# Channel-mix and convolution scan: group statistics over 64 rows at once, rows normalised four at a time

## The reference

```
x = x + mix(gn(x))          # gn: group norm, 32 groups of 2 channels, eps 1e-5
x = x + scan(gn(x))

mix:  posmap = softmax over n of pos_score[m, n, s]        # 4 heads s
      out[b,w,m,v,s] = sum_n posmap[m,n,s] * x[b,w,n,v,s]  + token_bias[m]
scan: out[0] = row[0]
      out[h] = row[h] + relu(conv1d(out[h-1], W))          # h = 1..63, 9 taps, 64 -> 64 channels
```

## Time and profile before

| | us |
|---|---|
| median of 3 runs (875.48 to 876.52) | 876.46 |
| the profiled execution | 875.68 |
| its span in the trace | 873.6 |
| PE / PEld busy | 799.9 / 732.1 |
| ACT busy | 642.9 |
| DVE busy | 618.7 |
| POOL busy | 435.7 |

### The profile page before, as it was taken

One profiled execution on the slowest core, in us unless ns is written; L12 is line 12 of the kernel. 1 busy time (PEld: TensorE's weight loads), 2 busy tenths in 40 slices (PEclk: granted clock), 3 DMA queues, 4 the chain that ended last, 5 costly groups with the idle time before them and its releaser, 6 DMA issues.

```text
span 873.6 us, 20141 instructions
## 1 busy us (share of the span) xinstructions
PE 799.9 (92%) x5734; PEld 732.1 (84%) x5734; DVE 618.7 (71%) x1536; ACT 642.9 (74%) x1462; POOL 435.7 (50%) x416
## 2 busy tenths in 40 slices
PE   1778887888799999999999999997999999999997
PEld 1555555555599999999899999997999999999997
DVE  7677778777578888989797978765555555555553
ACT  2477777777758887888788888887677677677664
POOL 1665655566265655566566665662333333333333
PEclk9999999999999999999999999999999999999999
DMA  9334343433134444444434343221222222223223
GB/s 186 68 74 96 74 96 72 90 78 83 38 74 93 90 97 98 98 90 94 90 84 91 87 96 74 49 50 37 62 62 67 66 60 67 65 60 68 64 60 72
DMA packets 203159, 68.18 MB, mean 78 GB/s; under 512 B 137556, under 2 KB 203092, under 8 KB 203092
## 3 DMA queue, kind: packets, MB, share of 16 engines
q1 hardware_dynamic: 203092, 67.43, 35.0%
HBM read 33.85 MB, written 33.55 MB: 77 GB/s over the span
## 4 chain that ended last, share of the span: by engine, by line
PE 71%; issue 9%; ACT 7%; DVE 7%; POOL 3%; ACTq 1%; DMA 1%; SPq 1%; DVEq 0%; POOLq 0%
PE ps_conv L898 30%; PE ps_conv L902 15%; PE ps_mix L812 8%; PE ps_mix L814 6%; PE ps_out L890 5%; ACT x_paired L424 5%; PE ps_in L827 5%; PE ps_small L801 2%; POOL xs L341 2%; POOL total L364 1%; DVE carry L732 1%; DVE x_sb L642 1%; DVE st L553 1%; DVE st L649 1%; DMA x_sb<-in_x_dram 1%
## 5 line engine op out<-in xcount | busy, mean ns | idle before, releaser
L364 POOL TENSOR_TENSOR total<-x_paired,carry 128x256 f32<-128x256 f32 x256 | 193.5, 757 | 299.6 <-DVE carry L732 293.5
L341 POOL TENSOR_TENSOR xs<-x_sb,rstd 128x512 f32<-128x512 f32 x128 | 232.9, 1846 | 93.6 <-DVE rstd L624 66.8
L424 ACT ACTIVATE x_paired<-ps_in,shift 64x256 f32 (+1 forms) x512 | 237.9, 465 | 7.8 <-POOL total L364 1.2
L740 DVE TENSOR_TENSOR carry_l<-carry,carry_h 128x256 fp32r<-128x256 f32 x252 | 177.0, 703 | 86.3 <-ACT carry_h L483 83.7
L898 PE MATMUL ps_conv<-carry_h,wh 128*128 128x256 f32 x1280 | 219.7, 303 | 4.7 <-ACT carry_h L483 4.7
L463 ACT ACTIVATE rows<-x_paired,shift,rstd 128x128 f32 (+1 forms) x512 | 221.3, 481 | 0.9 <-DVE shift L672 0.7
L483 ACT ACTIVATE carry_h<-carry 128x256 fp32r<-128x256 f32 x252 | 105.8, 420 | 140.9 <-DVE carry L732 139.0
L898 PE MATMUL ps_conv<-carry_h,wl 128*128 128x256 f32 x1280 | 197.7, 285 | 0.0
L902 PE MATMUL ps_conv<-carry_l,wh 128*128 128x256 f32 x1280 | 196.8, 284 | 0.0
L898 PEld LDWEIGHTS ps_conv<-carry_h,wh 128*128 128x128 f32 x1280 | 176.9, 192 | 7.2 <-ACT carry_h L483 5.6
L898 PEld LDWEIGHTS ps_conv<-carry_h,wl 128*128 128x128 f32 x1280 | 174.0, 190 | 0.0
(11 more groups left out here) (73 smaller groups left out, 354.9 us busy)
## 6 DMA issues: line engine op xcount, KB each, us to landing
x_sb<-in_x_dram SPq DMA_DIRECT2D x64, 512.0 KB, 4.0
out_dram<-staged SPq DMA_DIRECT2D x256, 128.0 KB, 2.4
x_paired<-in_L_conv_W_dram SPq DMA_DIRECT2D x2, 80.0 KB, 2.7
x_paired<-in_L_conv_W_dram SPq DMA_DIRECT2D x2, 64.0 KB, 2.4
x_paired<-v_attention_centers_dram SPq DMA_DIRECT2D x1, 0.0 KB
x_paired<-v_attention_spreads_dram SPq DMA_DIRECT2D x1, 0.0 KB
bias_col<-v_token_proj_n_bias_dram SPq DMA_DIRECT2D x1, 0.5 KB, 5.3
```

What stands on the lines that cost most here:

```text
L341: nc.gpsimd.tensor_tensor(xs[:, c % 2, heads, :, :], src, rstd1[:, m:G:2].unsqueeze(1).unsqueeze(1).to_broadcast([P, CG, CR, V]), ALU.mult ...
L364: nc.gpsimd.tensor_tensor(total[s][:, :].rearrange("p (w j) -> p w j", w=WS), x1_rows(wave, it, i, 1, s * WS, WS)[:, 0, :, :], carry[s][:, ...
L424: ins = nc.scalar.activation(dst[q * C:(q + 1) * C, r:HR:2, :], src[:, q, :, :], ACT.Identity, bias=shift1[r * C:(r + 1) * C, e:e + 1])
L740: nc.vector.tensor_tensor(carry_l[s][:, :, EDGE:EDGE + J], carry[s][:, :].rearrange("p (w j) -> p w j", w=WS), carry_h[s][:, :, EDGE:EDGE ...
```

## The change

Statistics of `x` are taken over all 64 rows in 16 operations of 256 elements; all stand in steps 4 and 5, two in each gap, and for image 0 behind the softmax. The tiles lose their dimension of halves, each average on PE has one source instead of two, and the matrix holds 1/128 instead of 1/256. Rows are normalised four at a time (`RG` = 4): one operation of 256 elements behind each `carry_h` instead of two of 128, and `rows` holds twice as much. The load of chunk 3 moves from step 2 to step 1.

```diff
-    RG = 2
+    RG = 4
-    HALF_COUNT = H // 2 * CG
+    COUNT = H * CG
...
-                    if i in (0, 2) and more >= 1:
-                        load_chunk(b + 1, 1 - e, 2 + i // 2)
+                    if i in (0, 1) and more >= 1:
+                        load_chunk(b + 1, 1 - e, 2 + i)
...
-                            for k in range(2):
-                                norm_rows(wave, it + g // GROUPS, g % GROUPS, (i % RG) * 2 * NS + 2 * s + k)
+                            norm_rows(wave, it + g // GROUPS, g % GROUPS, (i % RG) * NS + s)
...
-            def stats1(b, e, half, first, count):
-
-                for c in (2 * half, 2 * half + 1):
+            def stats1(b, e, first, count):
+
+                for c in range(CH):
                     dve.wait_ge(x_loaded[e][c], 8 * (b - e) + 16)
-                v = x_sb[:, e, 2 * half * CC:2 * (half + 1) * CC]
-                v = v.rearrange("p (h m g e) -> p m h e g", m=G // 2, g=2, e=CG)
+                v = x_sb[:, e, :].rearrange("p (h m g e) -> p m h e g", m=G // 2, g=2, e=CG)
                 for m in range(first, first + count):
-                    ins = nc.vector.bn_stats(st1[:, half, 2 * m:2 * m + 2, :].rearrange("p g k -> p (g k)"),
+                    ins = nc.vector.bn_stats(st1[:, 2 * m:2 * m + 2, :].rearrange("p g k -> p (g k)"),
                                              v[:, m, :, :, :])
-                if half == 1 and first + count == G // 2:
+                if first + count == G // 2:
                     ins.then_inc(stats1_done, 1)
...
-            stats1(0, 0, 0, 0, G // 2)
             dve.wait_ge(prob_ready, S)
...
-            stats1(0, 0, 1, 0, G // 2)
+            stats1(0, 0, 0, G // 2)
...
-                nc.vector.tensor_tensor(dev[:, :, :], st1[:, :, :, 1],
-                                        mean1.unsqueeze(1).to_broadcast([P, 2, G]),
-                                        ALU.subtract).then_inc(dev_ready, 1)
+                nc.vector.tensor_tensor(dev[:, :], st1[:, :, 1], mean1, ALU.subtract).then_inc(dev_ready, 1)
...
-                if more and i < 4:
-                    stats1(b + 1, 1 - e, 0, 4 * i + gap, 1)
                 if more and 4 <= i < 6:
-                    stats1(b + 1, 1 - e, 1, 8 * (i - 4) + 2 * gap, 2)
+                    stats1(b + 1, 1 - e, 8 * (i - 4) + 2 * gap, 2)
...
-                average(mean1, inv256[:, :], [st1[:, half, :, 1] for half in range(2)], mean1_ps)
+                average(mean1, inv_p[:, :], [st1[:, :, 1]], mean1_ps)
...
-                average(var1_ps, inv256[:, :], [m2[:, half, :] for half in range(2)], var1_in_ps)
+                average(var1_ps, inv_p[:, :], [m2[:, :]], var1_in_ps)
```

More of the change, by code:

```diff
@@ L78, in mix_and_scan_kernel @@
         ident = sb("ident", [P, P])
[L79 to L82, removed]
+        st1 = sb("st1", [P, G, 3])
+        dev = sb("dev", [P, G])
+        dev2 = sb("dev2", [P, G])
+        m2 = sb("m2", [P, G])
         var1 = sb("var1", [P, G])
@@ L100, in mix_and_scan_kernel @@
         half_power = sb("half_power", [P, 1])
-        inv256 = sb("inv256", [P, P])
+        inv_p = sb("inv_p", [P, P])
         minus_avg = sb("minus_avg", [P, 1])
@@ L538, in _ @@
             nc.vector.memset(ones_row, 1.0)
-            nc.vector.memset(inv256[:, :], 1.0 / (2 * P))
+            nc.vector.memset(inv_p[:, :], 1.0 / P)
             nc.vector.memset(minus_avg[:, :], -1.0 / P)
@@ L597, in deviations1 @@
                 dve.wait_ge(mean1_ps, b + 1)
-                nc.vector.tensor_tensor(dev[:, :, :], st1[:, :, :, 1],
-                                        mean1.unsqueeze(1).to_broadcast([P, 2, G]),
-                                        ALU.subtract).then_inc(dev_ready, 1)
+                nc.vector.tensor_tensor(dev[:, :], st1[:, :, 1], mean1, ALU.subtract).then_inc(dev_ready, 1)
                 dve.wait_ge(dev_ready, b + 1)
-                nc.vector.tensor_tensor(dev2[:, :, :], dev[:, :, :], dev[:, :, :], ALU.mult).then_inc(dev2_ready, 1)
+                nc.vector.tensor_tensor(dev2[:, :], dev[:, :], dev[:, :], ALU.mult).then_inc(dev2_ready, 1)
                 dve.wait_ge(dev2_ready, b + 1)
-                nc.vector.scalar_tensor_tensor(m2[:, :, :], dev2[:, :, :], float(HALF_COUNT), st1[:, :, :, 2],
+                nc.vector.scalar_tensor_tensor(m2[:, :], dev2[:, :], float(COUNT), st1[:, :, 2],
                                                ALU.mult, ALU.add).then_inc(m2_ready, 1)
@@ L608, in variance1 @@
                 dve.wait_ge(var1_in_ps, b + 1)
-                nc.vector.tensor_scalar(var1[:, :], var1_ps, 1.0 / HALF_COUNT, EPS, ALU.mult,
+                nc.vector.tensor_scalar(var1[:, :], var1_ps, 1.0 / COUNT, EPS, ALU.mult,
                                         ALU.add).then_inc(var1_ready, 1)
```

## The result

| | us | ratio to before |
|---|---|---|
| before, median | 876.24 | |
| after, median of 13 runs (877.26 to 880.01) | 878.44 | 1.0029, interval 1.002 to 1.0037 |
| the profiled execution after | 879.65 (span 877.5) | |

The change makes the kernel slower by 2.2 us by the medians and 2.5 by the ratio, 0.29%: small, but clear of the interval. The direction was forecast, the size (8.5 us) was not.

The account below looks back on a forecast made before the run. PE, busy 799.9 of 873.6 us, was taken as the bound; 875.68 plus start 1.0, turns 0.3 and 0.9, and first scan 6.3 (0.9 for each of 7 images) gave 884.2 us. Own range 880 to 889; 8 in 10, 875.0 to 890.0.

Parts of the forecast that it names:

- Prices: Operation costs: 256-element statistics 0.416 us alone, 0.33 in a row; 256-column row normalising on ACT 0.53 in a row.
- start: Image 0: all 16 larger statistics wait for the last chunk, partly offset by fewer PE passes; net +1.0 us.
- first stage: Images 0 to 7, no scan: two chains of equal length meet, so shortening one gives nothing; 0 us.
- second scan: PE is busy for all of its 131.00 us, so less ACT or DVE work cannot shorten it; 0 us.
- load: Chunk 3 loaded in step 1 instead of 2: data come earlier than steps 4 and 5 need; 0 us.
- The turns: Before each scan ACT normalises all eight images' first rows, twice as many per operation; +0.3 and +0.9 us.
- step 6 of the first scan: Second carry of step 5 is five gaps, 1.35 us, late, so POOL's sum reaches PE late; +0.5 us an image.
- the scan's sum in the table above: First scan's forecast by steps over seven images: -1.8 in 1 and 3, +1.9, +2.1, +3.9 in 5, 6, 7; +6.1 us.
- step 5: First scan: PE's output transposes wait for POOL's sum, whose carry of step 4 is one gap late; +0.27 us an image.
- step 7: First scan: POOL's sum 1.4 us late against a PE 0.8 late; +0.55 us an image.
- Rival 2: First scan: lateness costs about what is saved, +0.1 us an image; 878.7 us, or 877.5 if the start is free; chance 0.18.
- the third delay: The 0.55 us after 0.27 and 0.5 in the first scan; rival 2 had DVE's waits of steps 6 and 7 swallow it.

Follow-up runs that it names:

- e6: e5 with image 0's statistics taken in halves again, the first while chunks land, and four passes for its two averages; 869.74 us, ratio 0.9936.
- e1: Kernel before with only the rows normalised four at a time, one scratch tile shared to make room; 874.02 us, ratio 0.9980.
- e2: Kernel after with rows normalised two at a time again, so only the statistics are changed; 880.67 us, ratio 1.0055 to before.
- e11: e5 with rows normalised two at a time again; 873.35 us, ratio 0.9974 to before.
- e5: Kernel after with the first scan's statistics spread 2, 1 and 1 a gap over steps 3, 4 and 5; 870.58 us, ratio 0.9948 to before.
- e9: e2 with ACT's square root of the next image's variance moved ahead of the two row operations in step 7; 878.19 us, ratio 1.0033 to before.
- e3: Kernel after with each average taking its source twice at half weight, so PE has four passes again; 881.66 us, ratio 1.0061 to before.
- e7: Kernel after with chunk 3 loaded in step 2 again; 878.12 us, ratio 1.0029 to before.
- e8: e6 with six useless float32 matmuls on PE in the waits of each turn into a scan; 867.27 us, ratio 0.9911 to before.

## Why the forecast was wrong in size

**Prices, start, first stage, second scan, load: right.** +1.0 at the start measured 1.17 (e6: 1.1 back). The first stage's two equal chains held. The turns were forecast at +0.3 and +0.9. The second:

```profile
606.56 4.04 ACT L463 ACTIVATE rows<-x_paired,shift,rstd 128x256 f32<-128x256 f32 x8
...
609.29 0.16 DVE L667 SCALAR_TENSOR_TENSOR shift<-mean_kept,rstd 128x1 f32<-128x1 f32 x1 [0.66 <-POOL rstd L347]
...
611.56 1.14 PEld L891 LDWEIGHTS ps_conv<-carry_h,wh 128*128 128x128 f32 x5 [3.21 <-ACT carry_h L483]
611.56 1.43 PE L891 MATMUL ps_conv<-carry_h,wh 128*128 128x256 f32 x5 [3.12 <-ACT carry_h L483]
```

Eight row operations end at 610.60 where the last shift is written at 609.45: the turn, from the last carry of the first scan to the first of the second, took 11.99 for 11.41, +0.6. In the first turn the carry came 0.90 after the last shift for 0.79, +0.1.

**The step that failed: step 6 of the first scan, "+0.5".** The forecast added the gaps' 0.27 us up and had the second carry of step 5 1.35 late. The same places after:

```profile
350.03 0.42 DVE L725 SCALAR_TENSOR_TENSOR carry<-ps_conv,rows 128x256 f32<-128x256 f32 x1 [1.26 <-PE ps_conv L895]
...
352.11 0.84 DVE L733 TENSOR_TENSOR carry_l<-carry,carry_h 128x256 fp32r<-128x256 f32 x1
...
354.45 0.73 DVE L551 BATCH_NORM_STATS2 st<-x_sb 128x6 f32<-128x256 f32 x2
355.11 0.61 DVE L733 TENSOR_TENSOR carry_l<-carry,carry_h 128x256 fp32r<-128x256 f32 x1
...
360.27 0.44 DVE L725 SCALAR_TENSOR_TENSOR carry<-ps_conv,rows 128x256 f32<-128x256 f32 x1
...
362.56 0.40 DVE L725 SCALAR_TENSOR_TENSOR carry<-ps_conv,rows 128x256 f32<-128x256 f32 x1
```

From the first carry of step 4 the second carry of step 5 stands at 10.24 us against 9.22: 1.02 late. Each gap did grow by 0.27, as 354.45 to 355.11 is 0.66. But in gap 2 of both steps there was already a wait. Before:

```profile
350.13 1.17 DVE L740 TENSOR_TENSOR carry_l<-carry,carry_h 128x256 fp32r<-128x256 f32 x1
...
352.54 0.47 DVE L553 BATCH_NORM_STATS2 st<-x_sb 128x6 f32<-128x128 f32 x2
353.10 0.71 DVE L740 TENSOR_TENSOR carry_l<-carry,carry_h 128x256 fp32r<-128x256 f32 x1
```

Two statistics from 352.54 should have ended 0.39 later, and the split came 0.56 later, because it waits for ACT's copy. The brackets show no wait so short, and I had read their absence as "no idle time". That hid 0.17 of the increment in either step; the one of step 5 comes only behind the carry asked for. The split of step 4's first stream, held up by POOL, shrank from 1.17 to 0.84, 0.33 where one increment of 0.27 was forecast, and the next split from 0.71 to 0.61. Six increments of 0.27 less 0.33, 0.17 and 0.10 are the 1.02. The sum then:

```profile
360.88 0.74 POOL L364 TENSOR_TENSOR total<-x_paired,carry 128x256 f32<-128x256 f32 x1 [2.89 <-DVE carry L725]
...
366.77 0.72 POOL L364 TENSOR_TENSOR total<-x_paired,carry 128x256 f32<-128x256 f32 x1 [0.51 <-DVE carry L725]
```

It ends at 361.62. PE's rows, where the forecast's 0.5 should be:

```profile
355.49 0.44 PE L883 MATMUL ps_out<-ident,total 128*128 128x128 f32 x2 [0.28 <-POOL total L364]
...
361.37 0.75 PE L883 MATMUL ps_out<-ident,total 128*128 128x128 f32 x4
...
364.64 0.31 PE L794 MATMUL ps_small<-st,inv_p 128*128 128x32 f32 x2
...
366.68 0.38 PE L883 MATMUL ps_out<-ident,total 128*128 128x128 f32 x2
367.55 0.44 PE L883 MATMUL ps_out<-ident,total 128*128 128x128 f32 x2 [0.49 <-POOL total L364]
```

The group at 361.37 takes 0.75 for 0.60. PE waits for the sums of the two streams one after the other, and its first two transposes need only the first stream's. That is 0.18 us of slack which I had in the code and left out. PE itself is 0.19 late here (361.37 from the carry at 350.03, for 359.46 from 348.31). Of the lateness of 1.02 less these 0.19, 0.58 of slack that was seen and 0.18 that was not, 0.1 to 0.2 reach PE, not 0.5. Over seven images PE's waits there grew by 0.8 us, not 3.5. That is 2.7 of the 4.9 us by which the scan's sum in the table above was too high; step 5, where each image waited 0.16 more and not 0.27, and step 0 are most of the rest.

In step 7 the forecast's 0.55 met 0.46 to 0.71, 0.63 on average, but partly by luck. It took the sum for 1.4 us late and PE for 0.8 late. In the image shown the sum ends 1.04 late (367.49 from 350.03, for 364.73 from 348.31) and PE's transposes start only 0.12 late, because step 6 had cost them nothing; the two errors nearly cancel.

**What was left out: ACT's time.** The forecast said that in steps 4 and 5 DVE is the late engine, which is true, and concluded that 0.3 us of ACT per half step is worth nothing. It did not follow ACT in the steps where DVE waits for it. e1, e2 to after and e11 to e5 put it at 1.8 to 2.3 us in all, turns included, where +1.2 was forecast; e9 shows that in step 0 it acts through the square root, which sets when POOL's scaled chunk is there for PE. How it saves 1.0 us in step 5 of e1 was not tried by itself and stays open.

Together: statistics +7.3 forecast and 4.8 measured (e2), rows +1.2 forecast and about -2 measured. Rival 2 had named the size, 878.7, with "the third delay is swallowed". It was the second that was swallowed, not the third; 878.7 came out near the measured 878.44 for another reason, by luck.

The profiled execution after is 4.0 us slower than the profiled one before, the medians 2.2. 0.8 of it lies in the first eight steps of the second scan (33.97 us for 33.17), where PE's half clock lasted longer. With the same code there they took 33.98 in e3 and 33.30 in e7, so that this part varies from one execution to the next and is not put down to the change. With the start's 1.2, the turns' 0.7 and the scan's 1.2 it makes up 3.9 of the 4.0.

## What to carry to other kernels

Fewer, larger operations save their fixed cost and are still a loss when they all fall where their data first allow them. Spread over three steps instead of two, the same instructions turned +0.29% into -0.52% (with the rows' part in both). When lateness is followed through several engines, the waits too short for the brackets and the first part of each consumer's work belong in the sum, and so does every engine whose load the change lowers, at each place where the next one waits for it.

## What the runs showed of the hardware

After PE's waits ahead of the second scan, the last of them 3.12 us, its clock was granted at half (0.50 from 611 to 616 us in the kernel after, 1.2 of 2.4 GHz): five matmuls took 1.27 to 1.43 us for 0.77 to 0.88 at the full clock, for some 4 us. Six useless matmuls in the 4.4 us of waits (in e6) kept the higher level at the second turn: the first eight steps took 31.83 us in e8 for 33.30 in e6. By the Trainium skill, "TensorE: Matmul & The Clock Gate", section "The HAM clock gate", the clock follows how busy PE has lately been, and idle stretches lose it; the two traces agree, with 31.83 for 33.30.
